# A depthwise convolution with group norm: the inverse root moved to GpSimd as a power, with a quarter of the sums taken a unit later

## The reference

```
g = v.reshape(B, 32, 12, H, W)
n = (g - mean(g)) / sqrt(var(g) + 1e-5)            # over channel of group, H, W
x_cat = concatenate([n, n[:, :, :-1, :]], axis=2)
out = x + conv(x_cat, weight (C, 1, 56, 1), groups=C) + bias
```

## Time and profile before

| | |
|---|---|
| median of three runs | 801.83 us (800.35 to 806.18) |
| the profiled execution | 799.6 us, its span 797.8 us |
| busy: TensorE, DVE, ACT, POOL | 690.0, 713.8, 673.1, 583.9 us |
| moved | 316.09 MB, mean 396 GB/s |
| granted TensorE clock | 0.998 |

### The profile page before, as it was taken

One profiled execution on the slowest core, in us unless ns is written; L12 is line 12 of the kernel. 1 busy time (PEld: TensorE's weight loads), 2 busy tenths in 40 slices (PEclk: granted clock), 3 DMA queues, 4 the chain that ended last, 5 costly groups with the idle time before them and its releaser, 6 DMA issues.

```text
span 797.8 us, 9115 instructions
## 1 busy us (share of the span) xinstructions
PE 690.0 (86%) x1920; PEld 557.9 (70%) x1920; DVE 713.8 (89%) x1602; ACT 673.1 (84%) x1029; POOL 583.9 (73%) x1110
## 2 busy tenths in 40 slices
PE   0599999898899888998988998888898989988895
PEld 0477877776677667776776777777776767776784
DVE  7899999998998899999989999999888999989962
ACT  6799998888889888898888898888887888897893
POOL 4688787777677667687777677677786777776775
PEclk9999999999999999999999999999999999999999
DMA  9979999999999999999999999999999999999956
GB/s 343 409 301 375 410 410 418 424 418 417 416 416 414 414 426 412 413 404 402 405 417 418 412 402 400 411 412 410 402 409 406 409 407 399 410 406 403 375 239 251
DMA packets 43784, 316.09 MB, mean 396 GB/s; under 512 B 12816, under 2 KB 12944, under 8 KB 14992
## 3 DMA queue, kind: packets, MB, share of 16 engines
q1 hardware_dynamic: 43728, 315.51, 97.4%
HBM read 161.32 MB, written 154.14 MB: 395 GB/s over the span
## 4 chain that ended last, share of the span: by engine, by line
DMA 41%; SPq 16%; DVE 16%; POOL 10%; ACT 8%; issue 6%; PE 2%; POOLq 0%
DMA xt<-x 29%; DVE st L311 9%; DMA out<-xt 8%; SPq L190 7%; SPq L172 7%; POOL xt L278 6%; ACT xn L387 6%; DVE xt L336 4%; DMA runs<-taps 3%; ACT kept L396 2%; PE conv L462 2%; DVE runs L320 1%; DMA xt<-wide 1%; SPq L179 1%; SPq L183 1%
## 5 line engine op out<-in xcount | busy, mean ns | idle before, releaser
L462 PE MATMUL conv<-xn,runs 128*128 128x448 f32 x1536 | 645.3, 567 | 38.4 <-ACT xn L387 36.7
L462 PEld LDWEIGHTS conv<-xn,runs 128*128 128x128 f32 x1536 | 514.1, 346 | 101.9 <-ACT xn L387 58.5
L278 POOL TENSOR_TENSOR xt<-xt,kept 128x448 f32<-128x448 f32 x384 | 436.7, 1144 | 97.8 <-ACT kept L396 97.4
L387 ACT ACTIVATE xn<-xt,shift,rstd 128x672 f32<-128x672 f32 x512 | 462.8, 942 | 44.6 <-POOL shift L272 44.6
L311 DVE BATCH_NORM_STATS2 st<-xt 128x6 f32<-128x336 f32 x1024 | 451.9, 494 | 54.1 <-DMA xt<-x 49.4
L336 DVE SCALAR_TENSOR_TENSOR xt<-conv,bias_all,xt 128x448 f32<-128x448 f32 x384 | 256.8, 669 | 18.0 <-PE conv L462 18.0
L396 ACT ACTIVATE kept<-conv,bias_all 128x448 f32<-128x448 f32 x384 | 234.2, 620 | 10.7 <-PE conv L462 9.8
L438 PEld LDWEIGHTS p_mean<-msum,neg_mean 128*128 128x128 f32 x128 | 19.5, 192 | 94.3 <-POOL msum L247 79.5
L438 PE MATMUL p_mean<-msum,neg_mean 128*128 128x8 f32 x128 | 25.2, 269 | 59.2 <-POOL msum L247 59.2
L377 ACT ACTIVATE std<-var,eps 128x8 f32<-128x8 f32 x64 | 19.3, 301 | 54.5 <-DVE var L326 54.0
L268 POOL TENSOR_TENSOR newt<-r 128x8 f32<-128x8 f32 x64 | 12.7, 198 | 49.9 <-DVE r L331 48.2
(11 more groups left out here) (29 smaller groups left out, 111.6 us busy)
## 6 DMA issues: line engine op xcount, KB each, us to landing
xt<-x SPq DMA_DIRECT2D x128, 672.0 KB, 7.5
out<-xt SPq DMA_DIRECT2D x128, 672.0 KB, 6.8
xt<-x SPq DMA_DIRECT2D x128, 336.0 KB, 7.6
out<-xt SPq DMA_DIRECT2D x128, 336.0 KB, 6.9
out<-xt SPq DMA_DIRECT2D x128, 168.0 KB, 12.0
xt<-x SPq DMA_DIRECT2D x124, 168.0 KB, 12.4
runs<-taps SPq DMA_DIRECT2D x32, 192.0 KB, 10.9
xt<-wide SPq DMA_DIRECT2D x4, 336.0 KB, 7.2
```

Of the source, the lines that this page charges most:

```text
L278: nc.gpsimd.tensor_tensor(cell, cell, kept_of(u, c), ALU.add).then_inc(pool_added, 1)
L387: ins = nc.scalar.activation(xn[:, n % NS, :, part], xt[0:P, n % XS, :, part], ACT.Identity, scale=rstd[:, n % RS, b:b + 1], bias=shift[:, ...
L462: nc.tensor.matmul(bank(c), lay[:, :, c], channel_of(xn, u % NS, c), start=True, stop=True).then_inc(conv_ready, 1)
```

## The change

- The root on ACT, the reciprocal on DVE, the table warm-up and their two semaphores are gone. POOL now does the whole inverse root: eps is added, a `tensor_tensor` with `pow` raises the sum to -0.5, and one Newton step and `shift` follow. That is seven POOL instructions in a row in place of six.
- The last four of the 16 `bn_stats` of a unit (`LATE = 4`) move into the next unit's turn, so they end just ahead of the second `take` of the unit two before the one they serve. `add_means` moves behind the first `add_x` of that unit, `deviations` behind the second, `mean` behind channel 4, `variance` behind channel 6, and `negmean` behind the second `evict`.
- Three half loads (`EARLY_RELOADS = 3`) are issued one store sooner than before at the start; all later ones keep their place.
- At the start ACT normalizes four parts of unit 0 ahead of the second `negmean`.

```diff
+LATE = 4
+EARLY_RELOADS = 3
...
-                    if u >= 1:
+                    i = u * HALVES + h
+                    if 1 <= i <= EARLY_RELOADS:
+                        load((i - 1) // HALVES + XS, (i - 1) % HALVES)
+                    if i - HALVES >= EARLY_RELOADS:
                         load(u - 1 + XS, h)
...
-            def newton(n):
+            def inverse_root(n):
                 r = n % RS
                 pool.wait_ge(var_ready, n + 1)
-                chained(nc.gpsimd.tensor_scalar(hv[:], var[:, r, :], EPS, -0.5, ALU.add, ALU.mult))
-                pool.wait_ge(r0_ready, n + 1)
-                chained(nc.gpsimd.tensor_tensor(newt[:], r0[:, r, :], r0[:, r, :], ALU.mult))
-                chained(nc.gpsimd.tensor_tensor(newt[:], newt[:], hv[:], ALU.mult))
-                chained(nc.gpsimd.tensor_tensor(newt[:], newt[:], three_halves[:], ALU.add))
-                chained(nc.gpsimd.tensor_tensor(rstd[:, r, :], newt[:], r0[:, r, :], ALU.mult))
+                chained(nc.gpsimd.tensor_scalar(v_eps[:], var[:, r, :], EPS, None, ALU.add))
+                chained(nc.gpsimd.tensor_tensor(r0[:], v_eps[:], minus_half[:], ALU.pow))
+                chained(nc.gpsimd.tensor_tensor(newt[:], r0[:], r0[:], ALU.mult))
+                chained(nc.gpsimd.tensor_tensor(newt[:], newt[:], v_eps[:], ALU.mult))
+                chained(nc.gpsimd.tensor_scalar(newt[:], newt[:], -0.5, 1.5, ALU.mult, ALU.add))
+                chained(nc.gpsimd.tensor_tensor(rstd[:, r, :], newt[:], r0[:], ALU.mult))
                 nc.gpsimd.tensor_tensor(shift[:, r, :], nmean[:, r, :], rstd[:, r, :], ALU.mult
                                         ).then_inc(coef_ready, 1)
...
-                newton(n)
-            add_means(LEAD_COEF)
+                inverse_root(n)
             nc.gpsimd.memset(xt[:, 5, :, :], 0.0).then_inc(slot_zeroed[5], 1)
...
                 add_x(u, ACT_CH[0])
                 if n < UNITS:
+                    add_means(n)
+                add_x(u, ACT_CH[1])
+                if n < UNITS:
                     deviations(n)
-                for c in ACT_CH[1:4]:
-                    add_x(u, c)
-                if n < UNITS:
-                    newton(n)
+                add_x(u, ACT_CH[2])
+                add_x(u, ACT_CH[3])
+                if n < UNITS:
+                    inverse_root(n)
                 add_x(u, ACT_CH[4])
-                if n + 1 < UNITS:
-                    add_means(n + 1)
                 add_x(u, ACT_CH[5])
...
-            def invert(n):
-                dve.wait_ge(std_ready, n + 1)
-                nc.vector.reciprocal(r0[:, n % RS, :], std[:, n % RS, :]).then_inc(r0_ready, 1)
...
+                begin = (u + LEAD_STATS) * ALL - LATE
                 for k, c in enumerate(DVE_CH):
-                    if u + LEAD_STATS < UNITS:
-                        stats(u + LEAD_STATS, ends[k - 1] if k else 0, ends[k])
+                    if u < UNITS - LEAD_STATS:
+                        stats(begin + ends[k], begin + ends[k + 1])
                     take(u, c)
...
-            def root(n):
-                act.wait_ge(var_ready, n + 1)
-                nc.scalar.activation(std[:, n % RS, :], var[:, n % RS, :], ACT.Sqrt, bias=eps[:, 0:1]
-                                     ).then_inc(std_ready, 1)
...
             negmean(0)
-            root(0)
+            normalize(0, 0, 4)
             negmean(1)
-            normalize(0, 0, 2)
-            root(1)
-            normalize(0, 2, BP)
+            normalize(0, 4, BP)
...
                 evict(u, ACT_CH[0])
+                if n < UNITS:
+                    normalize(n, 2, 4)
+                evict(u, ACT_CH[1])
                 if m < UNITS:
                     negmean(m)
                 if n < UNITS:
-                    normalize(n, 2, 4)
-                evict(u, ACT_CH[1])
-                if n < UNITS:
                     normalize(n, 4, 5)
                 evict(u, ACT_CH[2])
...
-                        if c == 2:
+                        if c == 4:
                             mean(n)
-                        if c == 5:
+                        if c == 6:
                             variance(n)
```

More of the change, by code:

```diff
@@ L98, in build @@
         avg_dev = sb("avg_dev", [P, P])
-        eps = sb("eps", [P, 1])
-        warm = sb("warm", [P, 1])
-        three_halves = sb("three_halves", [P, BP])
+        minus_half = sb("minus_half", [P, BP])
         st = sb("st", [P, RS, HALVES, BP, 6])
@@ L107, in build @@
         var = sb("var", [P, RS, BP])
-        std = sb("std", [P, RS, BP])
-        r0 = sb("r0", [P, RS, BP])
-        hv = sb("hv", [P, BP])
+        r0 = sb("r0", [P, BP])
+        v_eps = sb("v_eps", [P, BP])
         newt = sb("newt", [P, BP])
@@ L134, in build @@
         var_ready = sem("var_ready")
-        std_ready = sem("std_ready")
-        r0_ready = sem("r0_ready")
         coef_ready = sem("coef_ready")
@@ L236, in _ @@
                     chained(nc.gpsimd.memset(m[:, a:b:4], 0.0))
-            nc.gpsimd.memset(three_halves[:], 1.5).then_inc(consts_set, 1)
-            pool.wait_ge(consts_set, 2)
+            nc.gpsimd.memset(minus_half[:], -0.5).then_inc(consts_set, 1)
+            pool.wait_ge(consts_set, 1)
             nc.gpsimd.memset(xt[:, 4, :, :], 0.0).then_inc(slot_zeroed[4], 1)
@@ L302, in _, with stats @@
         def _(dve):
-            nc.vector.memset(eps[:], EPS).then_inc(consts_set, 1)
             nc.vector.memset(runs[:], 0.0).then_inc(runs_zeroed, 1)
-            def stats(n, k0, k1):
-                for k in range(k0, k1):
-                    h, b = k // BP, k % BP
+            def stats(first, last):
+                for at in range(first, min(last, UNITS * HALVES * BP)):
+                    n, h, b = at // (HALVES * BP), at // BP % HALVES, at % BP
                     if b == 0:
@@ L311, in stats @@
                     ins = nc.vector.bn_stats(st[:, n % RS, h, b, :], xt[0:P, n % XS, h, b * ROW:(b + 1) * ROW])
-                if k1 == HALVES * BP:
-                    ins.then_inc(stats_ready, 1)
+                    if h == HALVES - 1 and b == BP - 1:
+                        ins.then_inc(stats_ready, 1)
             def lay_out(g):
@@ L339, in _ @@
             ALL = HALVES * BP
-            stats(0, 0, ALL)
-            stats(1, 0, ALL // 2)
+            stats(0, ALL * 3 // 2)
             add_vars(0)
-            stats(1, ALL // 2, ALL * 3 // 4)
-            invert(0)
-            stats(1, ALL * 3 // 4, ALL)
+            stats(ALL * 3 // 2, ALL * 2)
             lay_out(0)
-            stats(2, 0, ALL // 2)
+            stats(ALL * 2, ALL * 5 // 2)
             add_vars(1)
-            stats(2, ALL // 2, ALL * 3 // 4)
-            invert(1)
-            stats(2, ALL * 3 // 4, ALL)
+            stats(ALL * 5 // 2, ALL * 3 - LATE)
             dve.wait_ge(bias_loaded, 16)
-            ends = (3, 6, 8, 11, 13, 16)
+            ends = (0, 3, 6, 8, 11, 13, 16)
             for u in range(UNITS):
+                begin = (u + LEAD_STATS) * ALL - LATE
                 for k, c in enumerate(DVE_CH):
-                    if u + LEAD_STATS < UNITS:
-                        stats(u + LEAD_STATS, ends[k - 1] if k else 0, ends[k])
+                    if u < UNITS - LEAD_STATS:
+                        stats(begin + ends[k], begin + ends[k + 1])
                     take(u, c)
@@ L361, in _ @@
                         lay_out((u + 1) // PER_GROUP)
[L362 to L366, removed]
+                    if k == 3 and u + LEAD_COEF < UNITS:
+                        add_vars(u + LEAD_COEF)
+                if u == UNITS - 1 - LEAD_STATS:
+                    stats(begin + ALL, UNITS * ALL)
         @block.scalar
@@ L400, in _ @@
                 nc.scalar.memzero(xt[:, n, :, :]).then_inc(slot_zeroed[n], 1)
-            act.wait_ge(consts_set, 2)
-            nc.scalar.activation(warm[:], eps[:], ACT.Sqrt)
             negmean(0)
-            root(0)
+            normalize(0, 0, 4)
             negmean(1)
-            normalize(0, 0, 2)
-            root(1)
-            normalize(0, 2, BP)
+            normalize(0, 4, BP)
             act.wait_ge(bias_loaded, 16)
@@ L415, in _ @@
                 evict(u, ACT_CH[0])
-                if m < UNITS:
-                    negmean(m)
                 if n < UNITS:
@@ L420, in _ @@
                 evict(u, ACT_CH[1])
+                if m < UNITS:
+                    negmean(m)
                 if n < UNITS:
@@ L426, in _ @@
                 evict(u, ACT_CH[3])
-                if m < UNITS:
-                    root(m)
                 if n < UNITS:
@@ L463, in convolve @@
                                  ).then_inc(conv_ready, 1)
-            pe.wait_ge(consts_set, 2)
+            pe.wait_ge(consts_set, 1)
             for n in range(LEAD_COEF):
```

## The result

The changed kernel takes 960.23 us (median of 4 runs, 956.03 to 962.12) against 802.94 us for the kernel before: a ratio of 1.1967, 95% interval 1.192 to 1.2014. I had said 814 us, 794 to 842. The direction was right and the size was not: 157 us were lost, not 12.

The account below looks back on a forecast made before the run. The DMAs (12.06 us a unit) bound the middle before; after, the ACT-POOL loop (12.19) would. 41 + 61 x 11.99 + 25.7 = 798.1, plus 12.6 for the power, 810.7; plus 2.2 to the median, said as 814 us, range 794 to 842.

Parts of the forecast that it names:

- the loop: ACT and POOL, each unit: 11.05 us before, 11.99 + (p - 0.20) after, 12.19 at p = 0.40, against the DMAs' 12.06.
- a step of 0.20: POOL's inverse root: the power taking the 0.20 us of its plain 128x8 neighbours, giving a 798.1 us span.
- p: Duration of the power on POOL, in every loop: between 0.20 and 1.63 us, taken as 0.40.
- my upper bound: POOL's whole Newton run of six instructions, 1.63 us, which a power should not exceed.
- my own slope of 63 times: The power's price counts in 61 loops and twice at the start: 6.3 us for each 0.1 us.
- the second rival: A dear power on POOL, p from 0.6 to 1.0: medians of 827 to 852 us, 3 to 6% slower; chance 0.22.
- my formula: Start: unit 1 begins at about 41 us instead of 43.72, plus (p - 0.20) twice.
- The early refills and the late sums: Refills fill at most 5.3 us of DMA gap, 42 to 66 us; `LATE` saves 1.8 us at the end, if DMA-bound.

Follow-up runs that it names:

- the cheap step: Changed kernel with the power replaced by a multiplication of the same operands, output wrong: 801.29 us, ratio 1.0005 to the kernel before.
- the filled wait: Changed kernel with three extra convolution-sized multiplications a unit on TensorE ahead of `mean`, into unused columns: 893.42 us, ratio 1.1151.
- the order alone: Changed kernel with the root back on ACT, the reciprocal on DVE and Newton on POOL: 802.3 us, ratio 1.0007 to the kernel before.
- the kernel with the power alone: Kernel before with the root as a power on POOL, root and reciprocal gone, nothing moved: 905.89 us, ratio 1.1306.

## Why the prediction was wrong

**The bound and the loop: right.** That ACT and POOL form a loop, that the coefficients gate it, that `variance` ahead of channel 7 stretches it to 11.99 us, and that unit 1 begins at about 41 us with a step of 0.20: the cheap step gave 11.98 and 41.05. That each microsecond of the power counts once in every unit was right too: the filled wait gave 13.45 everywhere, against 13.50.

**The price of the power: the step that failed first.** The prediction bounded p by 0.20 and 1.63 us and took 0.40, "nearer the low end because the fixed cost of an instruction is paid once for eight elements a partition". It is 1.667, four times as much and just over my upper bound. By my own slope of 63 times, 1.27 us more are 79.8 us. I had priced the whole bound at 892 us in the second rival and then left it out of the range with "nothing speaks for it but that a power is no plain step". That was reason enough: no row showed the operation, so neither end had more behind it than the other.

**The clock: the step that was missing.** For a dear power the prediction took the loop as the only effect. But a longer loop with the same work leaves TensorE waiting: mostly 2.6 to 2.8 us for the sums, ahead of `mean`, where it waited 0.3 to 0.7 before. The granted clock fell to 0.50 behind about two in three of these waits, the convolutions that followed were slower, and `variance` behind them stands on the loop. Over 61 units that is 61 x (14.45 - 13.48) = 59 us. The filled wait gave back 62.7 us of span between the profiled executions (954.2 to 891.5). So even with the exact price of the power the sum, a median of 894 us, would have been 66 us short. The Trainium skill, TensorE: Matmul & The Clock Gate, Part 1, says that the clock is gated to 1.2 GHz after idleness and restored by activity; in this the trace agrees, with 0.50 behind the wait that ended at 91.01 and 1.00 from 98 us on, in the same unit. But waits of the same length left the clock at 1.00 in other units.

**The rest.** 810.7 of forecast span, 79.8 for the power, 2.5 for the first step of the run (0.04 us, 63 times) and 59 for the clock make 952.0; the span measured is 954.2. The other 2.2 us are what is left of a later start (1.5) and a longer end (27.4 us for 25.7), less 1.0 because the undisturbed intervals are 13.48 and not 13.50. At the start I had overlooked one thing: `normalize(0, 0, 4)` stands ahead of `negmean(1)`, whose copy waited until 24.60 instead of 22.60, and unit 1's deviations with it. Unit 1 began at 45.51, where my formula with the measured power gives 44.0. With the cheap step, where normalizing starts earlier, the copy came at 23.11 and unit 1 at 41.05, so it cost next to nothing.

**The early refills and the late sums,** worth up to 5.3 and 1.8 us only if the DMAs are the bound, could gain nothing at 960 us. Where the DMAs were the bound again (the cheap step, the order alone) no gain was seen either: the gap did close, to a share of 0.97 with the cheap step, and the rate in the middle was 409 GB/s for 411, the last loops 11.98 us for 11.05. The late sums were never run by themselves; they stand in both of these kernels.

## What to carry to other kernels

Before a new kind of operation goes onto a loop that every unit passes, measure it alone at its real shape, or keep the whole of its bounds in the range. Look in the engine's written order for what really needs the result: moved ahead of one add, the same power cost 1% instead of 20%. And when a loop grows, look at where TensorE will wait: here the lower clock behind that wait cost 67 us beside the 90 of the growth itself, and a few useless multiplications in the wait gave it back. Where only 1% was missing, one such multiplication gave nothing.

## What the runs showed of the hardware

- The power on GpSimd costs 0.563 us for one column of 128 partitions and 0.158 us for each further one between 16 and 32 columns; both exponents tried cost the same (1.638 and 1.636 us for -0.5 and 2.0 on eight columns); a multiplication on eight columns takes 0.201.
- The clock fell behind a wait in one unit and not behind the same wait in another: in the changed kernel it fell to 0.50 behind 2.70 us at 91.01 and stayed at 1.00 behind 2.70 us at 64.04. In the kernel with the power alone it fell to 0.50 behind 1.81; in the one with the cheap step, with waits mostly of 1.2 to 1.4 us, the mean clock was 0.999. The length of the last wait does not decide it alone.
- Adding three multiplications a unit, 2.4 us of work for TensorE, made the changed kernel 67 us faster.
